# A recommender's lookups by one-hot products: nine of 26 fields on TensorE instead of eight, gathers let go more slowly, three row buffers

## The reference

```python
sp_emb = emb_tables[fidx, sp_input]                      # 2048 x 26 x 32
lin_vals = lin_tables[fidx, sp_input, 0]
lin_output = ds_input @ lin_w.T + lin_b + jnp.sum(lin_vals, axis=1, keepdims=True)
s = jnp.sum(sp_emb, axis=1)
bi_pooled = 0.5 * (s * s - jnp.sum(sp_emb * sp_emb, axis=1))
x = jnp.concatenate([bi_pooled, ds_input], axis=1)
h = jax.nn.relu(x @ w1.T + b1)
h = jax.nn.relu(h @ w2.T + b2)
out = jax.nn.sigmoid(h @ fw.T + fb + lin_output)
```

## Time and profile before

| | us |
|---|---|
| median of 3 runs | 466.59 (463.79 to 466.76) |
| the profiled execution | 468.15 |
| its span, from the first instruction to the last | 466.4 |

### The profile page before, as it was taken

How to read it: one execution, slowest core, us unless ns; L and a number is a source line. 1 busy time by engine, 2 the same in 40 slices (tenths; PEclk the granted TensorE clock), 3 DMA queues, 4 the chain that set the end, 5 groups by cost and what they waited for, 6 DMA issues and landing times.

```text
span 466.4 us, 5488 instructions
## 1 busy us (share of the span) xinstructions
PE 410.4 (88%) x1797; PEld 337.5 (72%) x1798; DVE 332.0 (71%) x358; ACT 258.5 (55%) x450; POOL 284.2 (61%) x309
## 2 busy tenths in 40 slices
PE   8999799799789779789799979979979759979977
PEld 5788578688678668678688858768868645647735
DVE  8869569669649749559739849567787678677733
ACT  6799836356645644744564654665376358542133
POOL 6657557557557547566566657557557557566740
PEclk9999899899899999899899988998999997999959
DMA  7611141111511104111050112411142101001100
GB/s 207 189 29 27 21 164 26 21 21 17 172 13 27 22 10 166 21 25 23 10 179 11 24 23 36 153 23 12 24 145 38 12 11 13 10 12 12 15 9 0
DMA packets 17124, 23.02 MB, mean 49 GB/s; under 512 B 6245, under 2 KB 16183, under 8 KB 16186
## 3 DMA queue, kind: packets, MB, share of 16 engines
q1 hardware_dynamic: 7560, 17.62, 11.7%
q0 software_dynamic: 9536, 5.05, 10.0%
HBM read 22.61 MB, written 0.04 MB: 49 GB/s over the span
## 4 chain that ended last, share of the span: by engine, by line
PE 29%; DVE 24%; another core or an unknown queue 20%; issue 17%; ACT 7%; DMA 1%; SPq 0%; DVEq 0%; ACTq 0%
PE cand L899 12%; PE cand L902 12%; DVE masked L492 8%; DVE gates L467 7%; DVE low L479 4%; DVE picks L552 2%; ACT gates L726 2%; DVE pick_sq L555 2%; ACT distance L718 2%; PE cand L946 1%; DMA stage<-tabs 1%; ACT high L693 1%; PE bank_b L921 1%; PE cand L956 1%
## 5 line engine op out<-in xcount | busy, mean ns | idle before, releaser
L373 POOL DMA_INDIRECT rows<-table,row_idx x293 | 278.3, 950 | 162.5 <-issue 75.8
L899 PE MATMUL cand<-high,gates 128*128 128x462 f32 x826 | 319.6, 387 | 20.9 <-issue 19.5
L902 PE MATMUL cand<-low,gates 128*128 128x462 f32 x826 | 317.5, 384 | 19.2 <-issue 19.1
L899 PEld LDWEIGHTS cand<-high,gates 128*128 128x128 f32 x826 | 161.5, 196 | 53.0 <-issue 32.7
L902 PEld LDWEIGHTS cand<-low,gates 128*128 128x128 f32 x826 | 161.0, 195 | 45.8 <-issue 27.7
L492 DVE TENSOR_TENSOR masked<-cand,mask 128x924 f32<-128x924 f32 x58 | 64.8, 1117 | 92.5 <-remote 89.1
L500 DVE TENSOR_REDUCE picks<-masked 128x66 f32<-128x924 f32 x56 | 106.8, 1908 | 1.9
L726 ACT ACTIVATE gates<-distance,one 128x512 fp32r<-128x512 bf16 (+1 forms) x128 | 83.7, 703 | 10.9 <-remote 10.9
L718 ACT ACTIVATE distance<-codes,minus_key 128x512 bf16<-128x512 f16 (+1 forms) x119 | 77.8, 704 | 0.1
L706 ACT COPY bank_b<-high 128x462 f32<-128x462 f32 x47 | 25.8, 549 | 92.3 <-issue 61.3
L467 DVE TENSOR_SCALAR gates<-bank_a,key_of 128x512 fp32r<-128x512 f32 (+1 forms) x82 | 56.1, 736 | 1.1 <-issue 1.1
(11 more groups left out here) (114 smaller groups left out, 124.2 us busy)
## 6 DMA issues: line engine op xcount, KB each, us to landing
stage<-tabs SPq DMA_DIRECT2D x7, 1617.0 KB
rows<-table,row_idx POOLq DMA_INDIRECT x293
codes<-codes_dram SPq DMA_DIRECT2D x27, 128.0 KB
stage<-tabs SPq DMA_DIRECT2D x7, 231.0 KB, 2.9
idx_raw<-sparse SPq DMA_DIRECT2D x1, 208.0 KB
w_sb<-w2t SPq DMA_DIRECT2D x1, 128.0 KB
dense_sb<-dense_cols SPq DMA_DIRECT2D x1, 120.0 KB
x_and_y<-dense_rows SPq DMA_DIRECT2D x1, 112.0 KB
```

What stands on the lines that cost most here:

```text
L373: pool.indirect_dma_start(out=to, out_offset=None, in_=table[:, :], in_offset=bass.IndirectOffsetOnAxis(ap=row_idx[:, at:at + 1], axis=0), ...
L899: first = nc.tensor.matmul(to, gate, high[f % 2][:, k, :], start=(k == 0), stop=False)
L902: last = nc.tensor.matmul(to, gate, low[f % 2][:, k, :], start=False, stop=(k == CHUNKS - 1))
```

## The change

One field more, the ninth, goes to TensorE: `MMF` is 9, the jobs are 34 (fields 0 to 7 for all blocks, field 8 for tiles 8 to 11, 14 and 15), with 134 tiles of TensorE and 282 gathers. `LET` lets 1.10 + 0.86 = 1.96 gathers go per tile in the middle jobs, 7.84 a job. `RING` is 3. `TILE_AT` is spread over the longer row of jobs. The rest makes room in the memory or follows from 9 x 16 = 144 rows of codes: these lie as 72 x 256, `idx_wrap` is gone (its first use goes to a mask buffer that is still free, its second is in place), and the idle tile is 128 columns wide and read with a step of zero.

```diff
@@ -57,7 +57,7 @@
-    RING = 4
+    RING = 3
@@ -102,7 +102,7 @@
-    TILE_AT = {2 * t + 2: t for t in range(TILES - 5)}
+    TILE_AT = {2 * t + 2 + (t + 1) // 4: t for t in range(TILES - 5)}
     TILE_AT[NJ - 7] = TILES - 5
@@ -134,7 +134,7 @@
-    LET_OF = [[30, 30, 30, 440, 40, 40, 40, 340]] + [[135, 101] * TB] * (NJ - 5) + [[175] * 8, [175] * 8, [150] * 8, [280] * 4]
+    LET_OF = [[30, 30, 30, 440, 40, 40, 40, 340]] + [[110, 86] * TB] * (NJ - 5) + [[130] * 8, [130] * 8, [120] * 8, [280] * 4]
@@ -169,7 +169,6 @@
-        idx_wrap = sb("idx_wrap", [P, TILES * F], i32)
@@ -177,10 +176,10 @@
-        col_raw = sb("col_raw", [R, P], i32)
-        col_wrap = sb("col_wrap", [R, P], i32)
-        col_hi = sb("col_hi", [R, P], i32)
-        col_code = sb("col_code", [R, P], fp16)
+        col_raw = sb("col_raw", [R // 2, 2 * P], i32)
+        col_wrap = sb("col_wrap", [R // 2, 2 * P], i32)
+        col_hi = sb("col_hi", [R // 2, 2 * P], i32)
+        col_code = sb("col_code", [R // 2, 2 * P], fp16)
@@ -188,7 +187,7 @@
-        idle = sb("idle", [P, N], bf16)
+        idle = sb("idle", [P, P], bf16)
@@ -314,7 +313,7 @@
-            sp.dma_start(codes_dram, col_code[:, :]).then_inc(codes_out, 16)
+            sp.dma_start(codes_dram.rearrange("(r k) p -> r (k p)", k=2), col_code[:, :]).then_inc(codes_out, 16)
@@ -400,13 +399,14 @@
-                nc.vector.tensor_scalar(idx_wrap[:, :], idx_raw[:, :], 0, CATS, ALU.is_lt, ALU.mult).then_inc(idx_step, 1)
+                wrap = masked[1][:, :, :].rearrange("p t m -> p (t m)")[:, 0:TILES * F]
+                nc.vector.tensor_scalar(wrap, idx_raw[:, :], 0, CATS, ALU.is_lt, ALU.mult).then_inc(idx_step, 1)
                 dve.wait_ge(idx_step, 1)
-                nc.vector.scalar_tensor_tensor(idx_wrap[:, :], idx_raw[:, :], last_row[:, 0:1], idx_wrap[:, :], ALU.min,
+                nc.vector.scalar_tensor_tensor(idx_raw[:, :], idx_raw[:, :], last_row[:, 0:1], wrap, ALU.min,
                                                ALU.add).then_inc(idx_step, 1)
...
@@ -982,7 +982,7 @@
-                    nc.tensor.matmul(spare, idle[:, 0:P], idle[:, :], start=True, stop=True)
+                    nc.tensor.matmul(spare, idle[:, :], idle[:, 0:1].broadcast_to([P, N]), start=True, stop=True)
@@ -1105,7 +1105,7 @@
-    P, M = 128, 8
+    P, M = 128, 9
@@ -1123,7 +1123,7 @@
-        "cols": np.ascontiguousarray(sp[:, :M].T).reshape(M * (B // P), P),
+        "cols": np.ascontiguousarray(sp[:, :M].T).reshape(M * (B // P) // 2, 2 * P),
```

More of the change, by code:

```diff
@@ L408, in other_rows @@
                 nc.vector.scalar_tensor_tensor(
-                    row_idx[:, F:].rearrange("p (t f) -> p t f", f=F), idx_wrap[:, F:].rearrange("p (t f) -> p t f", f=F),
+                    row_idx[:, F:].rearrange("p (t f) -> p t f", f=F), idx_raw[:, F:].rearrange("p (t f) -> p t f", f=F),
                     0, field_base[:, :].unsqueeze(1).broadcast_to([P, TILES - 1, F]), ALU.max, ALU.add).then_inc(idx_set, 1)
@@ L435, in find_subs @@
                 nc.vector.tensor_scalar(sub_hi[:, :].rearrange("p (t f) -> p t f", f=MMF),
-                                        idx_wrap[:, :].rearrange("p (t f) -> p t f", f=F)[:, :, 0:MMF], 0, CATS - 1,
+                                        idx_raw[:, :].rearrange("p (t f) -> p t f", f=F)[:, :, 0:MMF], 0, CATS - 1,
                                         ALU.max, ALU.min).then_inc(sub_step, 1)
```

## The result

The changed kernel took 448.64 us in the median (445.67 to 452.97) against 466.63 for the kernel before: a ratio of 0.962, 95% interval 0.958 to 0.967. The forecast was 523 us with a range of 506 to 531; it was wrong in sign. The ratios leave out runs more than 1.5% above the fastest of their kernel. A second and a third pair, in other sessions, gave 0.961 (0.954 to 0.969; 448.96 against 466.07 us) and 0.965 (0.958 to 0.972; 447.27 against 463.82).

The account below looks back on a forecast made before the run. TensorE was taken to set the pace. The profiled 468.15 us plus 56.7 for four more jobs with stalls and 0.3 for reductions gave 525.2; the median of the runs lies 1.56 lower, so 523 us, range 506 to 531.

Parts of the forecast that it names:

- TensorE sets the pace: Middle stretch, jobs 2 to 25: the other engines follow TensorE, at 14.17 us a job, 11.80 us without stalls.
- 224 products at 0.2107 us, 47.2 us: Four more full jobs on TensorE: extra products at the undisturbed pitch, covered by nothing, cost 47.2 us.
- The stalls, 4 x 14.17 = 56.7 us: TensorE's middle jobs: stalls continue, so each of four new jobs costs what old ones cost, 56.7 us in all.
- the first of its two bounds: TensorE's stalls come with its work or time: 56.7 us more, 523 us in all; chance 0.56.
- the second bound: TensorE's stalls come with gathers and shrink to 55.2 us: the change costs 45.6 us, 512 us in all; chance 0.27.
- So a gather alone makes no stall.: From 102.26 us GpSimd gathers at full rate while TensorE is busy 22.00 of 22 and 24.00 of 24 us.
- The ring of three: Three row buffers: tile t + 3 waits until tile t is reduced; least slack 1.7 jobs, 20 to 24 us, cost nothing.
- the fewer sums: VectorE: each tile's sum has one gathered row less; reductions over nine fields cost 0.3 us, bounds 0 and 1.
- the start: Column codes on 72 partitions add about 0.6 us, covered by some 1.3 us of slack: zero, at worst 1 us.
- The instruction transfers: 14 transfers of 16 KB, TensorE's instruction stream: more products mean more of it, which would again be the first bound.
- The end stretch, "the last 94 us alike": After the middle jobs, four jobs mixed with the small network: 94 us, expected alike in the new profile.
- Rival D: Gathers collide with TensorE or what feeds it; at 1.96 a tile the collisions end: 457 us, faster; chance 0.04.

Follow-up runs that it names:

- prompt session: No kernel change: one of three sessions where TensorE's semaphore posts were seen 0.02 us after their product; the kernel before took 387.9 us.
- small edits: Kernel after with eight fields, 298 gathers and the pace of before, keeping three row buffers and memory layout: 388.66 us prompt, 459.18 us held.
- held: No kernel change: one of five sessions where TensorE's semaphore posts came late and in batches; the kernel before took 459 to 467 us.
- few posts: Kernel before with 6 semaphore posts of TensorE in a job in place of 16, same gathers and products: 388.15 us prompt, 465.27 us held.
- lumped kernel: Kernel after with middle jobs' gathers let go in lumps of 15.7 every second job, same average number: 435.21 us prompt, 558.21 us held.

## Why the prediction was wrong, point by point

- **TensorE sets the pace.** Right in a prompt session, where a middle job of the small edits took 11.78 us. In a held one the statement was half of the truth: TensorE was itself stopped by the gathers. 24 x 9.44 = 226 gathers in 340.0 us is 0.665 a us, and no kernel with this pace did much better when held (229 in the kernel before once more, 230 with the small edits and 230 with the few posts, from 32 to 372 us). GpSimd's pauses of 3 us after 12 gathers are, as I read the traces, part of a loop: a train holds the posts, the posts are GpSimd's own permits, so it stops, the batch comes, and the next train starts.
- **224 products at 0.2107 us, 47.2 us.** Right. The middle job took 11.91 us against 11.80. In the prompt session the lumped kernel stood 47.3 us above the kernel before (435.21 - 387.88).
- **The stalls, 4 x 14.17 = 56.7 us.** This is the step that failed. I chose the first of its two bounds, that stalls come with TensorE's work, and both were wrong: the total went from 56.8 us to 333.4 - 28 x 11.80 = 3.0 us. It does not scale with gathers either. What the runs showed in its place is that tight trains of gathers stop TensorE, in held sessions, with an edge: 1.96 gathers a tile give trains of 8 to 10, just short of the length at which TensorE stops; 2.36 give 12. The edge lies close: of 14 trains of 10 in the middles of the three held traces of the kernel after, five end in a stall, 13.1 to 13.5 us after their start. (In the second bound 56.8 x 220 / 226 is 55.3 and not 55.2 us; nothing hangs on it.)
- **"So a gather alone makes no stall."** I read the earlier trace rows as evidence against the gathers: TensorE ran through while GpSimd issued at its full rate. The windows ended at 114.0 and 342.5 us, and the stalls came at 115.65 and 343.71, at the ends of the trains from 102.3 and 330.0. I had cut the windows by where TensorE was busy, which chooses the parts of trains that are still harmless.
- **The ring of three, the fewer sums, the start.** Nothing on the path, as costed: 459.18 against 459.36 us for the small edits held, 388.66 against 387.88 prompt. The start was 2.0 us shorter in the profile, but in the three held traces of the kernel after it took 30.1, 30.1 and 32.3 us and in two of the kernel before 32.1 and 32.7, so part of that at least is chance.
- **The instruction transfers.** They did not separate the cases: 14 in the kernel before, with stalls, 14 with the small edits in the prompt session, without, and 16 after.
- **The end stretch, "the last 94 us alike".** Wrong: 80.3 us. It looks like the same cause, for with the small edits this stretch took 89.5 us held and 73.7 us prompt; no run takes it apart from the new pace of the last jobs.
- **Rival D** named the right mechanism, gathers that collide with what feeds or frees TensorE, and its point of decision: 83% of the stalls had to go; in the middle 95% went (56.8 to 3.0 us). It gave 457 us, 8 us too much; the end stretch, which it left alone, is the rest. I gave it 0.04, on the strength of the windows above.
- The view that would have shown it was on hand: the idle times of GpSimd's timeline, twelve gathers and a gap of 3 us, again and again, each train's end beside a stall.

What stays open: what in the chip holds the posts, and by what way that stops TensorE, which waits for none of them; whether it is the mean pitch of a row that counts or its pauses; why some sessions do not show it.

## What to carry to other kernels

When an engine stops between instructions that wait for nothing, lay its stalls beside the timelines of all other engines, from one pause to the next and not over windows chosen by the engine itself, and ask for a repeating count before calling the cause unknown. Gathers issued back to back from GpSimd are worth limiting to trains of at most 9, or some 11 us, where a kernel shows such stalls, or worth spreading: here a mean of 1.43 us did no harm over 15 of them. Before keeping a change that trades one engine's work for another's, time both kernels on several chips and at several times: here the trade is a gain of 4% in one kind of session, and in the other its products alone, with the gathers in lumps, are a loss of 12%.

## What the runs showed of the hardware that was not expected

- One program, 387.9 us in three sessions and 459 to 467 in five, chip 0 once among either, with the same gather pitch (1.25 us), product pitch (0.21 us) and arrival of a gather's last packet (median 1.2 us after its issue ended in either kind).
- TensorE's semaphore posts seen 0.02 us after the product in the one kind; in the other held during tight trains of gathers, up to 11 us in the train shown, and released together after the train's last gather ended: in the median 2.5 us after it in the kernel before, 1.9 in the kernel after, 2.8 with the lumps.
- In the same held session, no post held through 15 gathers at a mean of 1.43 us.
- TensorE stopping 12.8 to 14.9 us into a train at 1.25 us a gather, with 6 or 16 posts in a job, and 15.0 to 18.1 us at 1.34, and creeping until the posts are released; the granted clock then falls to 0.5 for some us. Over the whole execution it was 0.951 before, 1.000 after and 0.898 with the lumps.
- A fill of 64 columns on GpSimd (0.17 us) behind each gather costs 0.03 us, because it lies in the gap of 0.30 us that is there anyway.
